# Q, K, V and gate projections as three products of rounded 32-bit parts, tokens normalised on GpSimd, and three waits moved behind the second pass of the prologue

## What is computed

```python
xn = _layernorm(x)                                   # x: (4, 1024, 256)
Q, K, V = (proj_split(w, bias) for ...)              # xn @ w.T + bias, 16 heads of 16
S = einsum('hid,hjd->hij', K, Q) * SCALE             # causal, with a linear decay
attn = softmax(S) @ V                                # then @ o_w.T + o_b
probs = softmax(xn @ gate_w)                         # 8 experts, top 2 of them
s, g = attention output, silu(mixture of experts)
out = x + s * g
```

## Time and profile before

| | |
|---|---|
| median of 3 runs | 728.95 us (727.36 to 729.01) |
| profiled execution, its own time | 730.94 us |
| its span | 728.4 us |
| chunks 0 to 7 and the gap between them | 10.1 to 129.6 us of the span |
| PE busy over the span | 96% |
| DVE / ACT / POOL busy | 72% / 68% / 29% |
| mean granted clock of TensorE | 0.987 |

### The profile page before, as it was taken

How to read it: one execution, slowest core, us unless ns; L and a number is a source line. 1 busy time by engine, 2 the same in 40 slices (tenths; PEclk the granted TensorE clock), 3 DMA queues, 4 the chain that set the end, 5 groups by cost and what they waited for, 6 DMA issues and landing times.

```text
span 728.4 us, 17257 instructions
## 1 busy us (share of the span) xinstructions
PE 696.7 (96%) x5911; PEld 446.8 (61%) x5914; DVE 526.1 (72%) x1130; ACT 496.2 (68%) x1019; POOL 214.2 (29%) x300
## 2 busy tenths in 40 slices
PE   8899999999999999999999999999788999999975
PEld 4455455555555565555555555654367899989864
DVE  5425776999999989989998999896233564444298
ACT  4546452577777887877787778878775666666374
POOL 3200000135013333423333332300034757566300
PEclk9989999899999999999999999999999999999999
DMA  6999956314745675487478557710358677865297
GB/s 195 272 276 296 346 171 179 120 35 92 132 102 137 154 160 148 129 166 162 129 148 178 135 130 163 166 27 23 96 123 231 240 209 214 222 192 182 105 395 253
DMA packets 77206, 124.44 MB, mean 171 GB/s; under 512 B 14184, under 2 KB 47464, under 8 KB 77000
## 3 DMA queue, kind: packets, MB, share of 16 engines
q1 hardware_dynamic: 68368, 98.32, 52.8%
q0 software_dynamic: 8752, 25.02, 10.6%
HBM read 72.56 MB, written 49.72 MB: 168 GB/s over the span
## 4 chain that ended last, share of the span: by engine, by line
PE 80%; DVE 9%; DMA 6%; SPq 2%; ACT 1%; issue 1%; POOL 0%; POOLq 0%; DVEq 0%; ACTq 0%
PE ps L1532 19%; PE ps L1465 14%; PE ps L1516 12%; PE ps L1413 7%; PE ps L1620 7%; PE ps L1642 7%; PE ps L1454 6%; DVE mxa L1070 4%; PE ps L1420 4%; DMA arena<-xs_dram 3%; PE ps L1603 2%; DVE x_room L1379 1%; DVE arena L1374 1%; DVE arena L1364 1%; PE ps L1405 1%
## 5 line engine op out<-in xcount | busy, mean ns | idle before, releaser
L1070 DVE TENSOR_REDUCE mxa<-ps 128x1 f32<-128x512 f32 (+3 forms) x608 | 358.5, 654 | 45.4 <-PE ps L1454 27.0
L941 ACT ACTIVATE arena<-ps 128x512 f32<-128x512 f32 x576 | 303.5, 602 | 82.2 <-PE ps L1516 41.4
L1465 PE MATMUL ps<-aug 57*128 57x512 f32 (+3 forms) x768 | 217.9, 401 | 2.3 <-DVE mxa L1070 0.4
L1516 PE MATMUL ps<-aug 59*128 59x512 f32 (+3 forms) x768 | 215.9, 399 | 0.5 <-ACT arena L941 0.5
L1532 PE MATMUL ps<-arena,v_q 128*32 128x512 f32 (+3 forms) x1536 | 155.2, 499 | 6.7 <-ACT arena L941 6.3
L1516 PEld LDWEIGHTS ps<-aug 59*128 59x128 f32 x768 | 109.9, 186 | 76.1 <-ACT arena L941 69.0
L1465 PEld LDWEIGHTS ps<-aug 57*128 57x128 f32 x768 | 109.3, 186 | 46.4 <-DVE mxa L1070 31.1
L862 POOL DMA_INDIRECT y_dram<-arena,y_row_of x71 | 69.6, 981 | 54.8 <-DVE y_row_of L1303 45.9
L835 POOL DMA_INDIRECT xs_dram<-arena,slot x64 | 62.7, 980 | 73.1 <-ACT arena L941 69.5
L1454 PE MATMUL ps<-key_mask,key_rows 64*128 64x64 bf16 (+2 forms) x704 | 79.1, 208 | 0.0
L1620 PE MATMUL ps<-arena 128*128 128x128 f32 x568 | 75.3, 276 | 0.0
(11 more groups left out here) (143 smaller groups left out, 663.6 us busy)
## 6 DMA issues: line engine op xcount, KB each, us to landing
aug<-k_parts SPq DMA_DIRECT2D x96, 128.0 KB
aug<-q_parts SPq DMA_DIRECT2D x96, 128.0 KB
arena<-xs_dram SPq DMA_DIRECT2D x71, 128.5 KB, 2.6
k_parts<-arena SPq DMA_DIRECT2D x16, 512.0 KB, 4.9
q_parts<-arena SPq DMA_DIRECT2D x16, 512.0 KB, 7.4
arena<-y_dram SPq DMA_DIRECT2D x16, 512.0 KB, 6.7
xn_dram<-arena SPq DMA_DIRECT2D x8, 512.0 KB, 6.8
a_dram<-arena SPq DMA_DIRECT2D x128, 32.0 KB
```

What stands on the lines that cost most here:

```text
L941: nc.scalar.activation(prob_slot(q, i), score_bank(q, i), ACT.Exp).then_inc(exp_done, 1)
L1070: nc.vector.tensor_reduce(dst, src, AX.X, ALU.max).then_inc(piece_used, 1)
L1465: ins = nc.tensor.matmul(banks[:, at_ * width:(at_ + 1) * width], k_aug[n][rows, hp, ib * P:(ib + 1) * P], q_aug[n][rows, hp, lo:lo + widt ...
L1516: ins = nc.tensor.matmul(out_[:, col0:col0 + hi - lo], q_aug[n][rows, h // SIDES_OF_ARRAY, jb * P:(jb + 1) * P], k_aug[n][rows, h // SIDES ...
```

## The change

1. The weights and the transposed tokens are each split into a part rounded to fp32r and the rest of it, also fp32r (`wk_two`, `wq_two`, `wvg_two`, `xnT_high`, `xnT_low`). A product becomes high x high + low x high + high x low: `project` and `values` are six fp32r matmuls where they were two 32-bit ones. The parts lie in `split_room`, the room of the experts' weights, which are loaded later.
2. ACT makes the high parts of the weights, DVE the low part of K's, POOL the low parts of the others, all before or during chunk 0. DVE makes `xnT_low` (`take_low`), two instructions of 128x512 a chunk, and PE's second transposing half now waits for the first of them, since it is what frees bank 6.
3. Tokens of chunks 1 to 7 are normalised by POOL, not ACT. POOL's DMAs of the decays follow chunk by chunk.
4. Transposes stand in steps 1 and 2, not both in step 2; the statistics move from step 1 to step 0, `roots` from step 2 to step 1.
5. PE's waits for constants, masks and decays, and DVE's for the constants, move from ahead of chunk 2 to the first piece, in chunk 4.

```diff
+            pool.wait_ge(weights_in, 16 * len(WEIGHTS))
+            for n, (w, two) in enumerate(((wvg_sb, wvg_two), (wq_sb, wq_two))):
+                pool.wait_ge(weights_high, n + 2)
+                nc.gpsimd.tensor_tensor(two[1], w[:, :, :], two[0].bitcast(fp32), ALU.subtract).then_inc(weights_low, 1)
...
+            for i in range(1, CHUNKS * B):
+                b, c = i // CHUNKS, i % CHUNKS
+                pool.wait_ge(rstd_ready, i + 1)
+                pool.wait_ge(xpose_done, 2 * i)
+                pool.wait_ge(xn_out[c], 16 * b + 16)
+                for t in range(CT):
+                    ins = nc.gpsimd.tensor_scalar(xnb[c][:, t, :], xb[c][:, t, :], rstd[:, c, t:t + 1],
+                                                  shift[:, c, t:t + 1], ALU.mult, ALU.add)
+                ins.then_inc(xn_ready, 1)
+                if i <= AUG:
+                    load_decays(i - 1)
...
             roots(0)
-            normalise(0, 0, 0)
+            normalise_first()
+            act.wait_ge(key_in, 16 * len(KEY_WEIGHTS))
+            nc.scalar.activation(wk_two[0], wk_sb[:, :, :], ACT.Identity, scale=SCALE).then_inc(weights_high, 1)
             take_transposed(0, 0, 0)
+            act.wait_ge(weights_in, 16 * len(WEIGHTS))
+            nc.scalar.activation(wvg_two[0], wvg_sb[:, :, :], ACT.Copy).then_inc(weights_high, 1)
+            nc.scalar.activation(wq_two[0], wq_sb[:, :, :], ACT.Copy).then_inc(weights_high, 1)
...
+            def take_low(i, c, k, source):
+                dve.wait_ge(xT_ready, 2 * i + k + 1)
+                nc.vector.tensor_tensor(xnT_low[c][:, k, :], source, xnT_high[c][:, k, :].bitcast(fp32),
+                                        ALU.subtract).then_inc(xT_low, 1)
...
             def transposes(i, c, k):
                 if i > 0:
-                    pe.wait_ge(xT_ready, 2 * i + k)
+                    pe.wait_ge(xT_low, 2 * i + k)
...
-                for k in range(KT):
-                    ins = nc.tensor.matmul(bank(4 + n % 2), (wk_sb, wq_sb)[side][:, k, m * P:(m + 1) * P],
-                                           xnT[c][:, k, :], start=(k == 0), stop=(k == KT - 1))
+                for s, (w, xT) in enumerate(((weights[0], xnT_high[c]), (weights[1], xnT_high[c]), (weights[0], xnT_low[c]))):
...
+                    if s == 2 and n == 0:
+                        pe.wait_ge(xT_low, 2 * i + 2)
+                    for k in range(KT):
+                        ins = nc.tensor.matmul(bank(4 + n % 2), w[:, k, m * P:(m + 1) * P], xT[:, k, :],
+                                               start=(s == 0 and k == 0), stop=(s == 2 and k == KT - 1))
...
-            pe.wait_ge(consts_in, 16 * NCONST)
-            pe.wait_ge(masks_set, 4 * SIDES_OF_ARRAY)
-            pe.wait_ge(decays_in, 16 * 2 * SIDES_OF_ARRAY * AUG)
             ahead_of_windows = iter(list(enumerate(stream(0))))
...
                         s, item = next(ahead_of_windows)
+                        if s == 0:
+                            pe.wait_ge(consts_in, 16 * NCONST)
+                            pe.wait_ge(masks_set, 4 * SIDES_OF_ARRAY)
+                            pe.wait_ge(decays_in, 16 * 2 * SIDES_OF_ARRAY * AUG)
```

More of the change, by code:

```diff
@@ L166 @@
 HALF = CT // 2
+TRANSPOSE_AT = (1, 2)
 WARMING = 16
 AUG_AT = 16512
+EXPERTS_AT = AUG_AT + 4 * 2 * AUG * HP * T
 FIRST_BANK = (6, 3)
@@ L307, in attention_moe_kernel @@
         parts = [cut_parts()]
-        xnT = [cut(KT * BANK).rearrange("p (k t) -> p k t", k=KT) for _ in range(CHUNKS)]
         last_parts = at[0]
@@ L372, in attention_moe_kernel, with in_split @@
         k_aug = [aug[:, n, :, :] for n in range(AUG)]
+        def in_split(first, n, m=KT):
+            return split_room[:, first:first + m * n].rearrange("p (k n) -> p k n", n=n)
+        wk_two = [in_split(KT * D * s, D) for s in range(2)]
+        wq_two = [in_split(KT * D * (2 + s), D) for s in range(2)]
+        wvg_two = [in_split(KT * (4 * D + (D + E) * s), D + E) for s in range(2)]
+        xnT_high, xnT_low = [[in_split(KT * (4 * D + 2 * (D + E)) + KT * BANK * (CHUNKS * s + c), BANK) for c in range(CHUNKS)]
+                             for s in range(2)]
         q_aug = [aug[:, AUG + n, :, :] for n in range(AUG)]
@@ L878, in take_transposed, with normalise_first @@
                 act.wait_ge(xpose_done, 2 * i + k + 3)
-                nc.scalar.activation(xnT[c][:, k, :], bank(6), ACT.Copy).then_inc(xT_ready, 1)
-            def normalise(i, b, c):
-                act.wait_ge(rstd_ready, i + 1)
-                if i > 0:
-                    act.wait_ge(xpose_done, 2 * i)
-                act.wait_ge(xn_out[c], 16 * b + 16)
-                for t in range(HALF if i == 0 else CT):
-                    ins = nc.scalar.activation(xnb[c][:, t, :], xb[c][:, t, :], ACT.Identity,
-                                               bias=shift[:, c, t:t + 1], scale=rstd[:, c, t:t + 1])
+                nc.scalar.activation(xnT_high[c][:, k, :], bank(6), ACT.Copy).then_inc(xT_ready, 1)
+            def normalise_first():
+                act.wait_ge(rstd_ready, 1)
+                act.wait_ge(xn_out[0], 16)
+                for t in range(HALF):
+                    ins = nc.scalar.activation(xnb[0][:, t, :], xb[0][:, t, :], ACT.Identity,
+                                               bias=shift[:, 0, t:t + 1], scale=rstd[:, 0, t:t + 1])
                 ins.then_inc(xn_ready, 1)
@@ L1007, in statistics @@
                 dve.wait_ge(x_in[c], 16 * b + 16)
[L1008 removed]
+                if i >= CHUNKS:
                     dve.wait_ge(xn_ready, i - 1)
@@ L1043, in chunk @@
                     rest(i, c, n)
+                    if n in TRANSPOSE_AT and more > 0:
+                        take_low(i + 1, 1 - c, TRANSPOSE_AT.index(n), bank(6))
                     item(2 * n + 1)
-                    if n == 1 and more > 1:
+                    if n == 0 and more > 1:
                         statistics(i + 2, b + 1, c)
@@ L1418, in values @@
                 pe.wait_ge(v_out, 4 * i + t)
-                for k in range(KT):
-                    ins = nc.tensor.matmul(bank(7)[:, 0:D + E], xnT[c][:, k, t * P:(t + 1) * P], wvg_sb[:, k, :],
-                                           start=(k == 0), stop=(k == KT - 1))
+                if i == 0 and t == 0:
+                    pe.wait_ge(weights_low, 1)
+                for s, (xT, w) in enumerate(((xnT_high[c], wvg_two[0]), (xnT_high[c], wvg_two[1]), (xnT_low[c], wvg_two[0]))):
+                    for k in range(KT):
+                        ins = nc.tensor.matmul(bank(7)[:, 0:D + E], xT[:, k, t * P:(t + 1) * P], w[:, k, :],
+                                               start=(s == 0 and k == 0), stop=(s == 2 and k == KT - 1))
                 ins.then_inc(v_done, 1)
@@ L1428, in chunk @@
                     item(2 * n)
-                    if n == 2 and more > 0:
-                        transposes(i + 1, 1 - c, 0)
+                    if n in TRANSPOSE_AT and more > 0:
+                        transposes(i + 1, 1 - c, TRANSPOSE_AT.index(n))
                     values(i, c, n)
                     item(2 * n + 1)
-                    if n == 2 and more > 0:
-                        transposes(i + 1, 1 - c, 1)
             pe.wait_ge(zeros_set, 1)
```

52 lines of the change are left out of this document (28 added, 24 removed).

## The result

The changed kernel takes 726.07 us (median of 9 runs, 720.84 to 728.87) against 729.01 us (9 runs) of the kernel before: ratio 0.9931, 95% interval 0.9904 to 0.9958, faster by 0.7%. Beside the kernel before on another chip it was 0.9895 (0.9857 to 0.9933). 718 us was forecast, with 708 to 724 around it, so the direction was right and the size wrong. The attention windows start at 124.7 us instead of 129.7, so 5.0 of the 6.9 are the prologue's. The windows' stage took 405.1 us (404.7 before) and what lies behind it 191.7 us (194.0 before). No instruction was changed in either, and traces differ from run to run, so these 1.9 us aren't counted as the change's.

What follows compares the result with a forecast made beforehand. PE, busy 96%, was taken as the bound, with chunk 2's stores gating chunk 4. 5.5 + 1.2 + 2.2 + 2.1 = 11.0 us off 730.9 gave 719.9, median 2.0 lower: 718 us, range 708 to 724.

Steps and rivals of the forecast that it cites:

- What bounds the kernel, and the matmuls: PE, busy 96%; in the prologue six-matmul project 1.32 us, values 0.72, a step 0.56 us shorter, weight loads hidden.
- Chunks 5 to 7: Prologue chunks with 13 pieces each: savings of 1.2, 2.2 and 2.1 us, DVE holding chunk 5 at 15.2 us.
- Chunk 0: Start of prologue: PE stands about 2 us before its transposes; chunk 0 ends near 22.0 us, 0.4 later.
- Where that gain goes: Chunk 4: PE arrives 13.7 us ahead, but the gain isn't kept, as chunk 2's stores must land first.
- So the gate opens at 62.6 us: Chunk 4: chunk 2's stores landed at 62.6 us (60.6 to 65.7), 3.0 us sooner.
- Chunk 5 starts 5.5 us sooner: Prologue from the gate on: 3.0 sooner, 4.0 done ahead, -1.3 for banks, -1.5 for restart, +1.3 for cheaper matmuls.
- The 2 us: SP's DMAs behind chunk 0: most decays' DMAs come later, so masks get out sooner, 0 to 4 us, taken as 2.
- The 1 us: SP's queue: chunk 2's first store goes out ahead of SP's wait instead of behind it, 1.3 us, taken as 1.
- None of this starts sooner: SP and DMA chain ahead of chunk 4: its constants, stores and 12 loads don't start sooner because PE is faster.
- The restart: Chunk 4: PE restarts at half clock after some 8 us of idleness, costing 1.5 us, between 0 and 3.
- The gate stays where it is and the restart is cold: Rival, chance 0.15: chunk 4's gate doesn't move; 1.0 us there and some 4 in chunks 5 to 7, 724 us.
- The median: Whole kernel: the median of the runs lies 2.0 us below the profiled execution, so 719.9 becomes 718 us.

Runs made afterwards that it cites:

- statistics in step 2: Changed kernel with DVE's statistics and ACT's roots moved to step 2, behind both take_low: ratio 0.9945 to the kernel before.
- four buffers: Changed kernel with four buffers for x instead of two, so that chunk 5's x loads in chunk 1: ratio 0.9942 to the kernel before.
- x(5) ahead and late stores: Changed kernel, chunk 5's x loaded ahead of SP's wait for parts, normalised-token stores of chunks 1 to 3 put behind chunks 3 to 5: 733.96 us, ratio 0.9821.
- combined versions: Changed kernel with several edits: aug's first loads later plus four x buffers 0.9976, or plus later token stores 0.9889; later stores, earlier x, later statistics 0.988.
- late loads: Changed kernel with aug's twelve first loads issued behind chunk 2's stores and chunk 5's x ahead of them: 720.4 us, ratio 0.9869; on another chip 0.9882.
- x(5) ahead of the wait: Changed kernel with the load of chunk 5's x moved ahead of SP's wait for chunk 2's parts: 734.85 us, ratio 0.9838.

## Why the prediction was wrong

**What bounds the kernel, and the matmuls: right.** A project was forecast at 1.32 us and measured 1.40, a values at 0.72 and 0.74. Weight loads of 0.2 us over all rows stayed hidden. By the rule of the Trainium skill, "TensorE: Matmul & The Clock Gate", section "Part 3: Packing small matmuls — row/col tiling", that a weight load overlaps with matmuls in flight only where the row groups differ, they would not have. This trace disagrees: six matmuls and their six loads took 1.40 us.

**Chunks 5 to 7: right.** 5.5 us forecast, 5.8 measured (16.4 to 14.4, 17.2 to 15.3, 15.5 to 13.6), and DVE busy 14.18 us in chunk 5. DVE was to hold that chunk at 15.2 us; it did not, the chunk took 14.4. The kernel with full-precision matmuls gives it back, 130.7 against 124.7. DVE's wait for pieces, 13.8 us in the earlier trace rows, is 7.1 from 65 to 125 us.

**Chunk 0: right but for the clock.** It ends at 24.0, not 22.0. 1.6 to 1.9 us of that are the half clock behind the 2.2 us stall, which some executions have and some have not (22.1 to 22.3 without). The stall, forecast at about 2 us, is there with ACT's tokens too, so GpSimd isn't its cause.

**The failed step is "Where that gain goes": "So the gate opens at 62.6 us", and "Chunk 5 starts 5.5 us sooner".** Chunk 5 starts 0.9 us later. The gate was named rightly, chunk 2's parts, but its time was taken from before less 2 us for the masks and 1 us for a store that goes out sooner. The parts land at 67.3 us, 1.6 later than in the earlier trace rows.

The 2 us: SP issued the last mask at 31.5 us instead of 31.2, and chunk 1's first store at 31.8 instead of 32.6, 0.8 us sooner. Chunk 0 had ended 2.4 us later, and the late constants began at 25.4 us instead of 22.9. The 1 us: chunk 2's first store stood ahead of SP's wait before, too (issued at 42.74, the wait ended at 44.60). It goes out at 37.42 now, 5.3 us sooner, and landed at 47.0 instead of 46.5: a PE that makes parts sooner only puts them into full queues sooner. Chunk 1's last part was issued 0.5 us sooner and landed at 45.8 instead of 44.5. SP stood 7.1 us instead of 1.4 at that wait, and what is behind it went out later: the first load by 1.3 us, x(5) by 0.5, the last of chunk 2's parts by 1.4. x(5) landed 3.0 us later than before, the last part 1.7. "None of this starts sooner" was thought through; that some of it would end later was not.

Why chunk 1's last part landed later stays open. The DMA share was 1.08 from 36.2 to 43.2 us, but 0.58 in the 2.6 us before the landing. One rival is untested: the last four DMAs of the decays go out at 37.3 to 38.9 us now, where before all twelve had gone out by 22 us, and no version puts them back.

That this gate alone is enough to hold chunk 5 is shown by the version with the statistics in step 2, which keeps PE running through chunk 3 and still starts chunk 5 at 81.4 (the parts landed at 68.4 there). In the changed kernel x(5)'s chain holds it just as long, so neither gate can be called the only cause.

**Left out: the statistics behind chunk 0.** The change moves them from step 1 to step 0, ahead of `take_low`, and for chunks 1 to 3 the prediction gave that no price and no queue. They made a wait of 8.86 us for x(5) on DVE and so 9.02 us on PE. It lay in front of the parts' gate, so taking it away won nothing beyond chunk 0's clock in two versions (four buffers, statistics in step 2), but it hid the gate: ACT's first instruction of chunk 4 waits for PE, not for a DMA, against what the prediction said the profile would show. When the parts come sooner it counts.

**The restart: half clock as forecast, at another place.** It was forecast in chunk 4. It came in chunk 3, behind the 9.02 us: 5.60 us from the transposes to chunk 4 (60.53 to 66.13), where the same work took 3.33 us at full clock with x(5) ahead and late stores. These 2.3 us lie ahead of the parts' gate as well.

**The rivals.** "The gate stays where it is and the restart is cold" had 0.15 and 724 us, and comes nearest: the median was 726.07. That it comes so near is luck in part: its 5 us were 1.0 up to chunk 5 and 4 behind it, where -0.9 and 5.8 were measured. The gate was not even kept, it moved 1.6 us later. The 3 us by which the forecast moved it had no row of their own. The sum by its parts: 0.9 us lost up to chunk 5, 5.8 won behind it, 5.0 at the windows with rounding, where 11.0 were forecast.

**The median.** The forecast took the median 2.0 us below the profiled execution, as it was before. It came out 2.7 above it. So of the 8 us between 718 and 726.07, about 3.5 are the profiled execution's (723.35 against 719.9) and 4.7 this step's: one execution's distance from the median is no constant of a kernel.

**Where the rest of the gain lies.** Two mends, neither of which touches an engine's arithmetic, move chunk 5 from 81.4 to 72.4 us and the windows to 115.8: 118.6 was what the forecast hoped for. So the order of the DMAs and the late stores were what held the gain back. How the share of each splits is not shown, nor whether the stores count by their bytes or by the buffers that GpSimd waits for: the effects don't add, as the combined versions show.

## What to carry to other kernels

When transfers stand between a faster engine and the next stage, and their queues are already full, the gate need not move with the engine. Here it moved 1.6 us later, until the order of the transfers or the bytes ahead of it were changed (chunk 2's parts landed at 49.3 us with late loads). So a landing goes into the sum unchanged, or later, unless a row shows why it moves. Each instruction that a change moves on an in-order engine needs its own line in the sum: what it waits for, and what stands behind it. And count the bytes that nobody waits for (here 1.5 MB of stores that nothing in the prologue reads): behind the gate instead of ahead of it, and with buffers enough to keep them there, they gave 3.5 us more, from 119.3 to 115.8, where the matmuls' type gave 6.0.

## What the hardware showed that was not expected

- Two loads of one form, 512 KB of x, took 5.99 us from issue to landing when issued at 32.3 us (x(4) in the changed kernel) and 12.9 us when issued at 37.5 (x(5) ahead of the wait).
- A store of 512 KB issued 5.3 us sooner landed 0.5 us later (chunk 2's first part: 42.7 to 46.5 us before, 37.4 to 47.0 in the changed kernel).
- The same windows' instructions took 405.1 us on one chip and 421.2 us on another, at the same granted clock of 0.99. PE was busy 396.5 and 408.2 us of it. So versions on different chips can be compared only by their ratios to the kernel before.
- A fall to half clock for 3.4 us behind a stall of 2.3 us in chunk 0 came in one trace of the late-loads kernel and not in the other (chunk 0 ended at 23.9 and at 22.3 us), and the windows started 1.5 us apart.
- GpSimd's normalisation of 128x256 elements took 0.55 us, a little nearer to its copy (0.40) than to its operation with two inputs (0.73) in the earlier trace rows. The estimate was 0.45.
